# VectorE's order in a pair of units: the kernel before, and the change

## The reference

```python
h = relu(layernorm(x))                 # then inside the layer:
xn = layernorm(h) * ln_w + ln_b
w_phys = (silu(rbf @ w1 + b1) @ w2 + b2) * cutoff[:, None]
msg_phys = xn[col] * w_phys
Q, K, V = (xn @ wq + bq), (xn @ wk + bk), (xn @ wv + bv)   # 8 heads of 32
scores = sum(Q[row] * K[col], -1) / sqrt(32) * cutoff[:, None]
attn = softmax(scores, axis=1)         # over the 8 heads of one edge
combined = msg_phys + gate * (attn[..., None] * V[col])
aggr = segment_sum(combined, row, num_segments=n)
out = x + (h + aggr @ wo + bo)
```

## Time and profile before

| what | us |
|---|---|
| median of 3 runs | 5468.53 (5467.22 to 5485.16) |
| the profiled execution | 5472.01 |
| its span in the trace | 5470.3 |
| PE busy over the span | 5173.4 |
| DVE busy | 4191.7 |
| POOL busy | 3975.5 |
| ACT busy | 3927.3 |

### The profile page before, as it was taken

How to read it: one execution, slowest core, us unless ns; L and a number is a source line. 1 busy time by engine, 2 the same in 40 slices (tenths; PEclk the granted TensorE clock), 3 DMA queues, 4 the chain that set the end, 5 groups by cost and what they waited for, 6 DMA issues and landing times. The chain is left out here.

```text
span 5470.3 us, 117155 instructions
## 1 busy us (share of the span) xinstructions
PE 5173.4 (95%) x24352; PEld 3821.0 (70%) x24353; DVE 4191.7 (77%) x7424; ACT 3927.3 (72%) x12601; POOL 3975.5 (73%) x3476
## 2 busy tenths in 40 slices
PE   3779999999999999997799999999999999999999
PEld 3556666666666666675577777777777777777777
DVE  9789986666655655322788888888888888888894
ACT  4546666666666666665688888888888888888883
POOL 1567777777777777767578888888887888888880
PEclk9989999999999999998899999999999999999999
DMA  6233444444434444443999999999999999999956
GB/s 199 93 106 128 148 164 161 133 161 159 161 130 167 157 153 143 162 144 135 339 333 336 332 337 336 333 333 335 334 337 335 336 336 333 334 337 335 338 187 190
DMA packets 584400, 1306.16 MB, mean 239 GB/s; under 512 B 81246, under 2 KB 384134, under 8 KB 582961
## 3 DMA queue, kind: packets, MB, share of 16 engines
q0 software_dynamic: 221536, 881.08, 44.4%
q1 hardware_dynamic: 311796, 345.48, 21.1%
q10 hardware_dynamic: 50850, 77.03, 3.9%
HBM read 1024.15 MB, written 324.38 MB: 247 GB/s over the span
## 5 line engine op out<-in xcount | busy, mean ns | idle before, releaser
L1031 POOL DMA_INDIRECT ukvx<-kvx_table,urec x1760 | 2161.6, 1228 | 589.5 <-issue 532.0
L341 POOL DMA_INDIRECT records<-rows,slot_i x1660 | 1746.7, 1052 | 679.2 <-issue 470.1
L696 PE MATMUL w_ps<-w2s,hid 128*128 128x256 f32 x6656 | 1551.0, 387 | 51.7 <-DVE rows L610 51.5
L696 PEld LDWEIGHTS w_ps<-w2s,hid 128*128 128x128 f32 x6656 | 1247.7, 192 | 374.7 <-issue 156.2
L610 DVE TENSOR_TENSOR rows<-w_ps,b2b 128x512 f32<-128x512 f32 x832 | 571.5, 687 | 742.5 <-PE w_ps L696 742.2
L810 ACT ACTIVATE hid<-hid_ps,b1t 128x512 f32<-128x512 f32 x832 | 526.2, 683 | 817.6 <-PE hid_ps L685 802.8
L1153 PE MATMUL ag_ps<-ukvx,uonehot 128*128 128x256 f32 x3520 | 982.0, 402 | 0.2 <-issue 0.2
L1133 PE MATMUL uq_ps<-aggr,uonehotT 128*128 x3520 | 972.9, 399 | 2.1 <-ACT uonehotT L1048 1.0
L1158 PE MATMUL ag_ps<-ukvx,uonehot 128*128 128x256 f32 x3520 | 935.1, 388 | 24.6 <-issue 24.5
L1158 PEld LDWEIGHTS ag_ps<-ukvx,uonehot 128*128 128x128 f32 x3520 | 642.3, 190 | 191.6 <-issue 116.8
L1075 ACT ACTIVATE uexp<-uscores,umax 128x8 f32<-128x8 f32 x1760 | 507.4, 289 | 368.8 <-DVE umax L1239 365.7
(11 more groups left out here) (175 smaller groups left out, 5065.4 us busy)
## 6 DMA issues: line engine op xcount, KB each, us to landing
urec<-records SPq DMA_DIRECT2D x880, 260.0 KB, 6.1
rbf_in<-in_edge_attr SPq DMA_DIRECT2D x207, 256.0 KB, 3.0
kvx_table<-kvx ACTq DMA_DIRECT2D x10, 3456.0 KB, 14.5
ukvx<-kvx_table,urec POOLq DMA_INDIRECT x1760
records<-rows,slot_i POOLq DMA_INDIRECT x1661, 2.5
records<-kvx SPq DMA_DIRECT2D x1, 13000.0 KB
aggr<-query_table SPq DMA_DIRECT2D x7, 1792.0 KB, 19.2
fbase<-x_plus_h SPq DMA_DIRECT2D x14, 896.0 KB, 7.0
```

The lines of the kernel that those rows point to most:

```text
L341: pool.indirect_dma_start(recs, bass.IndirectOffsetOnAxis(ap=slot_i[:, q, t:t + 1], axis=0), rows[:, q, t, :], None).then_inc(scattered[q] ...
L696: m = pe.matmul(w_ps[j % 2][:, h, :], hid[:, k % 2, c, h, j * P:(j + 1) * P], w2s[:, c, :], start=(h == 0 and c == 0), stop=(c == 1), skip ...
L1031: pool.indirect_dma_start(kvx[:, k, j, :], None, table, bass.IndirectOffsetOnAxis(ap=rec[:, k, j, R_DST:R_DST + 1].bitcast(I32), axis=0), ...
```

## The change

`LAG` becomes 4 and `GATHER_AHEAD` becomes 6. VectorE's even step is now `query_key`, `attend` of the second pair behind, `maximum` of the pair behind. The odd step is `query_key`, `physical`, `score`, `invert` of the pair behind, `weigh`, `normalise` of the pair behind. `physical` loses its wait for the second gather, since `query_key` of both units now stands ahead of it. ScalarE takes the exponentials in the even step after the pair instead of in its odd step. The end of the loops is written out accordingly.

```diff
-LAG = 3
+LAG = 4
-        GATHER_AHEAD, SPREAD_AHEAD, TURN_AHEAD, OUT_AHEAD, ASK_AHEAD = 7, 5, 3, 2, 2
+        GATHER_AHEAD, SPREAD_AHEAD, TURN_AHEAD, OUT_AHEAD, ASK_AHEAD = 6, 5, 3, 2, 2
...
-                if k % 2:
-                    exponent(u, k, i, first)
+                if k % 2 == 0:
+                    behind(exponent, 1, u, k, i, first)
...
             turns(act, unit)
+            exponent(UNITS - 1, DEPTH - 1, TURNS - 1, False)
...
             def physical(u, k, i, first):
-                dve.wait_ge(kvx_in[k + 1], i * 32 + 32)
-                both = pair(kvx, k)[:, :, 2 * H:3 * H]
-                dve.tensor_tensor(both, pair(rec, k)[:, :, 0:H], both, ALU.mult).then_inc(s["phys_done"], 2)
+                both = pair(kvx, k - 1)[:, :, 2 * H:3 * H]
+                dve.tensor_tensor(both, pair(rec, k - 1)[:, :, 0:H], both, ALU.mult).then_inc(s["phys_done"], 2)
...
                 query_key(u, k, i, first)
                 if k % 2 == 0:
+                    behind(attend, 3, u, k, i, first)
+                    behind(maximum, 1, u, k, i, first)
+                else:
                     physical(u, k, i, first)
-                    behind(invert, 1, u, k, i, first)
-                    behind(normalise, 1, u, k, i, first)
-                    behind(attend, 1, u, k, i, first)
-                else:
                     score(u, k, i, first)
+                    behind(invert, 2, u, k, i, first)
                     weigh(u, k, i, first)
-                    maximum(u, k, i, first)
+                    behind(normalise, 2, u, k, i, first)
             turns(dve, unit)
-            U = UNITS
-            before = (U - 1, DEPTH - 1, TURNS - 1, False)
+            attend(UNITS - 3, DEPTH - 3, TURNS - 1, False)
+            before = (UNITS - 1, DEPTH - 1, TURNS - 1, False)
+            maximum(*before)
             invert(*before)
             normalise(*before)
             attend(*before)
```

## The result

| | us |
|---|---|
| before, median of 7 | 5473.28 |
| changed, median of 7 | 5525.08 (5497.99 to 5529.72) |
| ratio | 1.0081, 95% interval 1.0059 to 1.0103 |
| changed, the profiled execution | 5497.99, span 5496.3 |

Slower, as forecast, but by 44 us (0.81% of 5473; the medians lie 52 apart) and not by the 187 of the forecast. Of the seven, two lie at 5498 and 5501 us and five between 5520 and 5530; only the first has a trace, so what makes the others longer isn't shown.

A forecast was written before the change was run, and what follows sets the result against it. VectorE's own chain was taken to bound the kernel at 6.03 us a pair. 420 pairs x (6.60 - 6.15) = +189, plus 5 for start and drain, on 5472 gave 5666, rounded to 5660 us; range 5490 to 5800, wider 5385 to 5800.

The forecast's parts named there:

- VectorE's chain, 5.34 a pair: VectorE's instructions for two units, start to start: 6.03 us before, even step 1.93 plus odd step 3.41 after.
- TensorE holds at 5.74 if nothing else comes: TensorE, at 2.87 us a unit, becomes the limit; a pair would save 0.29 us.
- TensorE binds: Rival: GpSimd isn't held or catches up; 5.74 and 0.06 of edges a pair, 5320 us; chance 0.13.
- The waits priced at nothing: VectorE waits for TensorE, ScalarE, record loads or gather permission from later exponentials and new depths: nothing, or up to 0.3.
- Start and drain: Ends of the loop: one unit more at the end, 0 to 10 us, taken as +5.
- Only three gathers fit, GpSimd falls behind, `query_key` waits: GpSimd beside VectorE: `physical` and `attend` hold gathers, three pass per 5.74 us pair where four are needed; the lead shrinks.
- The pair in that state, 6.60: Pair time once `query_key` waits for gathers: four values from 6.11 to 7.16, mean 6.64, taken as 6.6 us.
- the landing of a gather: Time for a gather's data to land after GpSimd's instruction ends: 6.1 us, like record loads, to 6.9.
- the floor's 0.62: Least wait d ahead of the odd `query_key` that lets the second gather pass before `physical`; a pair is then 5.96 us.
- the walk: Following gathers from one end of `attend` to the next, all wait d before odd `query_key`: four per pair of 5.34 + d.
- No gain from standing apart: Rival: VectorE's 0.1 us gaps stay wherever instructions stand; a pair remains 6.03, about 5470 us; chance 0.03.
- Near the floor: Rival: gathers fall into a fixed beat, 5.96 to 6.10 a pair, -80 to -20, about 5415 us; chance 0.14.

The follow-up runs named there:

- e1: Changed kernel with `physical` and `attend` as reductions of the same 1024 elements reading one SBUF tensor, weighing left out: 5299.77 us, ratio 0.968.
- e3: Changed kernel's instructions reordered so `physical` and `attend` stand next to each other in the even step, all work done: 5300.33 us, ratio 0.9682.
- e5: Changed kernel with `physical` alone as a one-input reduction, weighing of messages left out: 5296.69 us, ratio 0.9669.
- e6: Changed kernel with `attend` alone as a one-input reduction, weighing of values left out: 5294.67 us, ratio 0.9672.
- e10: Changed kernel with `physical` and `attend` on 192 of 256 columns: 5300.57 us, ratio 0.9674.
- e7: Kernel before with `LAG` 4 and `GATHER_AHEAD` 6, VectorE's order as before: 5478.53 us, ratio 1.0004.
- e4: Changed kernel with all small instructions ahead of `attend` in the even step, `physical` and `score` in the odd step: 5496.40 us, ratio 1.0037.
- e9: Changed kernel with `physical` and `attend` on 224 of 256 columns: 5431.06 us, ratio 0.9918.
- e2: Kernel before with `physical` and `attend` turned into one-input reductions, weighing left out: 5470.92 us, ratio 1.0.

## Why the prediction was right, and where it was wrong

**VectorE's chain, 5.34 a pair.** Right within 0.08: it is 6.25 less 0.99 of idle time, 5.26. `normalise` starts 0.11 behind `weigh` and not 0.18.

**TensorE holds at 5.74 if nothing else comes.** Right: 5.74 in e1, e3, e5, e6 and e10, taken over units 60 to 870. The rival "TensorE binds" is what the same change gives where VectorE doesn't hold the gathers. Its price was 5320, these runs give 5295 to 5301. The rest is the 0.06 a pair that the rival added for the loop's edges: in these five traces the pair is 5.74 with the edges in it, and 420 x 0.06 is 25 us.

**The waits priced at nothing** (exponents a step later, record loads, `GATHER_AHEAD`, `LAG`). Right: e7 is at 1.0004, and e1 runs at TensorE's pace with all of them in it. Start and drain I set at +5; the start is -9 in the profiled execution.

**Only three gathers fit, GpSimd falls behind, `query_key` waits.** The mechanism was right. e1, e5 and e6 take it away and it goes, e3 moves it and it goes, e4 keeps the spacing and it stays. Full DMA engines, GpSimd by itself and the depths are excluded (e1, e3, e7).

**The pair in that state, 6.60.** Here the prediction failed: it is 6.24. Two terms of this step were mis-sized, the landing of a gather and the time for which a holding instruction shuts GpSimd out.

The landing I took as 6.1 to 6.9 us, from record loads and from a single gather early in the stage. In the changed kernel, from the end of a unit's second gather to the `query_key` that waited for it, it is 3.2 to 6.8 us with a median of 5.1, over the 393 waits of more than 0.15 us between 3005 and 5195 us. The gather of 4009.43 above ends at 4010.44, and the `query_key` of its unit is that of 4015.94. Put into the prediction's own formulas, 5.1 gives d = 0.27 for the gather that asked at 0, which is below the floor's 0.62, so 5.96 a pair, and d = 0.92 for the one that asked at 1.31, so 6.26. Their mean is 6.11, below the measured 6.24, where 6.1 to 6.9 had led to 6.6.

The other term I counted from the holding instruction's start to its end, 1.22 us, and added 0.11 for the small instructions with two inputs. On the trace of before this fits 1423 of 1423 gathers between 3005 and 5195 us, since there none ever asked within 0.30 us of the start of `physical` or `attend` or beside a small instruction. It couldn't tell. In the changed kernel it fits 975 of 1403. The misses tell the rule. Here a gather asks 0.16 us after `physical` starts, and isn't held:
```profile
3138.76 1.01 POOL L1031 DMA_INDIRECT ukvx<-kvx_table,urec  x1 [0.30 <-issue]
3138.74 1.27 DVE L1222 TENSOR_TENSOR ukvx<-urec,ukvx 128x1024 f32<-128x1024 f32 x1
```
Here one asks 0.18 us after it starts, and is held to its end:
```profile
3857.04 2.05 POOL L1031 DMA_INDIRECT ukvx<-kvx_table,urec  x1 [0.30 <-issue]
3857.00 1.22 DVE L1222 TENSOR_TENSOR ukvx<-urec,ukvx 128x1024 f32<-128x1024 f32 x1
```
77 gathers asked within 0.17 us of a start and passed. Of those that asked between 0.18 and 0.40 us after one, 118 in all, each was held. And this gather asks at 4002.00, while the small instructions run, and takes its 1.01, as do all 351 that asked beside a small one:
```profile
4001.86 1.01 POOL L1031 DMA_INDIRECT ukvx<-kvx_table,urec  x1 [0.30 <-issue]
...
4001.92 0.19 DVE L1234 SCALAR_TENSOR_TENSOR uscores<-uscores,urec 128x32 f32<-128x32 f32 x1
```
A rule that takes the holding instruction as a door, shut from 0.175 us after the start to the end, 1.05 us, and open beside small instructions, fits 1403 of 1403 in the changed kernel and 1344 of 1345 in e4, and the holding adds up to 346.8 us where 347.8 are measured. By the rule of the prediction it would be near 470. The small instructions need no rule of their own: they last 0.19 us, so a door that shuts after 0.175 is hardly shut at all.

What that does to the walk: the gather 1.31 us after the end of `attend` passes from d = 0.45 on instead of 0.62, and the one 2.62 us after the end of `physical` passes once the even `query_key` has waited about 0.25 us. The walk had that gather always held for 0.70, because it put the whole wait ahead of the odd `query_key`; the trace has more of it, 0.59 of 0.98, ahead of the even one.

How the miss of 0.36 a pair divides between the two terms is open. By the prediction's closed formulas it is the landing: with 6.1 to 6.9 all four values lie above the door's edge, and the later door changes none of them. Those formulas pick one gather by hand, though. Stepping the same recurrences over many pairs, with the durations of the rows and landings scattered by half a microsecond, is an estimate; no run shows its values. It gives 6.6 to 6.7 with the early door (shut from the start) and 6.3 to 6.4 with the late one (from 0.175 on), and about the same for any mean landing from 4.5 to 6.9. By it the door is most of the miss.

e9 and e10 were made to test the door, with 6.05 and 5.74 a pair for the late one and 6.4 and 6.1 for the early one. Over the stage e9 has 812 `query_key` in 2470 us, 6.08 a pair (the stretch of the group line above has 6.15), and e10 has 5.74:
```profile
L1218 DVE TENSOR_TENSOR ukvx<-uq_ps,ukvx 128x512 f32<-128x512 f32 x812 | 561.5, 692 | 439.7 <-DMA ukvx<-kvx_table,urec 406.5 <-PE uq_ps L1134 15.2 <-issue 11.5
```
The early door's times were out by 130 and 150 us. But the stepped values hang on the landing and its scatter (with a mean landing near 5 us the early door too can come out at 5.74 in e10), so the paces alone don't decide. The gathers do, one by one: between 3005 and 5195 us the late door fits 1443 of 1444 in e9 and 1503 of 1503 in e10, the early one 1059 and 1201.

**The rivals.** "No gain from standing apart", 5470, comes nearest in time, by chance: e1 against e2, 171 us, excludes its cause. "Near the floor" comes next, and its cause is wrong too: no fixed beat forms. That the time lies inside 5490 to 5800 is partly luck as well: 6.24 is just above the 6.2 with which the range began. Of the signs, the DMA share didn't fall under 0.93 (it is 0.95), and the wait stands more ahead of the even `query_key` than of the odd one. The Trainium skill, "VectorE: DVE Perf Modes", section "The DRAIN you can't avoid", has it that in a chain of copies measured there a semaphore after each costs nothing extra. Here the order alone, without the five gaps of the earlier trace rows, took VectorE's own chain from 6.03 to 5.26 us a pair, and the measurement decides. The Trainium skill, "SBUF — State Buffer", section "Who interferes with whom", names the contention, and the trace agrees with it for the instructions of 1024 elements: 347.8 us of holding in the changed kernel, none in e1. That the block lasts for the whole instruction holds here only from 0.17 us after the start that the profile shows.

## What to carry to other kernels

Where GpSimd issues gathers, place VectorE's long instructions with two SBUF inputs by the gathers' beat. Count how many gathers fit between them in one period of the loop; the same instructions gave 5300 and 5525 us by order alone. Before spreading dependent instructions out, look whether any engine that seems to have time to spare is being held by them. A rule read from a trace in a fixed beat is only tested at the phases that the beat visits, so give its edges a range of their own. And measure a latency on the transfers that will be waited for: the landing here was taken from record loads and a single gather, and came out at least 1 us too long.

## What the runs showed of the hardware

- What fits every gather looked at in the changed kernel (1403 of 1403): an indirect DMA of GpSimd needs what VectorE's instruction with two SBUF inputs holds only at one moment, 0.14 us after its start, and is held from 0.175 us after such an instruction's start to its end. Instructions of 32 elements (0.19 us) don't hold it (351 of 351).
- Where the gather comes first by little, VectorE pays: `physical` and `attend` then show 1.24 to 1.29 us instead of 1.22, as in the row of 3138.74.
- Two VectorE instructions with nothing to wait for overlap by 0.09 us at 1024 elements. One that reads what the one ahead wrote starts 0.19 to 0.20 us later than that.
- In e3 the DMA engines moved 359 GB/s at a share of 0.99 through the 2300 us from 2800 on, with gathers of rows of 3 KB, and nothing waited for them. A share of 0.96 wasn't a limit.
